# Adding the gated last row of v in the row tiles, by GpSimd from a broadcast half row, in a cross-attention and dense kernel

## What is computed

```python
q = layernorm(x);  k = v = ctx                       # 8 heads of 256 channels, 512 positions
corr = ifft(fft(q, positions) * conj(fft(k, positions))).real      # per channel
w, idx = top_k(corr, 12 per channel);  w = softmax(w)
out[pos] = sum_i w[i] * v[min(idx[i] + pos, 511)]    # per channel: shifted copies, clamped at the last row
x2 = x + tanh(g_xattn) * out
n = layernorm(x2)
base = n @ W_base.T + b_base
w_e = gates from softmax(n @ W_gate.T) and sigmoid(n @ W_thr + b_thr)
moe = (w_e * (n @ A_w[e].T)) @ B_w[e] summed over 8 experts, times 2
result = x2 + tanh(g_ffn) * (base + moe)
```

## Time and profile before

| | |
|---|---|
| median of 3 runs | 2907.98 us (2907.73 to 2909.68) |
| the profiled execution: its time / its span | 2908.95 us / 2907.1 us |
| busy: PE, PEld, DVE, ACT, POOL | 97%, 49%, 54%, 38%, 57% of the span |
| the attention's last output tiles end | at about 1318 us |
| first matmul of the first dense tile (L1146) | at 1381.65 us |
| mean granted clock of TensorE | 0.991 |

### The profile page before, as it was taken

The page is one execution under the profiler, slowest core; times in us unless marked ns, Lnnn a source line. Parts: engine busy times, 40 slices in busy tenths (PEclk is TensorE's granted clock), DMA queues, the critical chain, the costliest instruction groups (busy, mean ns, idle before and its releaser), DMA issues.

```text
span 2907.1 us, 35297 instructions
## 1 busy us (share of the span) xinstructions
PE 2815.5 (97%) x12932; PEld 1421.4 (49%) x12932; DVE 1559.7 (54%) x2646; ACT 1091.2 (38%) x1803; POOL 1661.9 (57%) x606
## 2 busy tenths in 40 slices
PE   5999999999999999987999999999999999999999
PEld 2454455555445555546444444444444444444444
DVE  5999999999999999996212112121212121212121
ACT  4666666666666664435211111111112121212110
POOL 4889898989898999950443343434242434333330
PEclk9999999999999999998999999999999999999999
DMA  5444445454444444347555454544444545445441
GB/s 199 131 131 125 131 138 143 145 145 140 121 122 136 134 131 116 102 160 259 167 169 159 148 155 159 152 161 149 159 144 160 152 158 157 153 159 156 148 131 44
DMA packets 264615, 424.97 MB, mean 146 GB/s; under 512 B 156271, under 2 KB 156847, under 8 KB 237109
## 3 DMA queue, kind: packets, MB, share of 16 engines
q1 hardware_dynamic: 245442, 288.93, 33.8%
q10 hardware_dynamic: 19068, 134.73, 13.4%
HBM read 256.79 MB, written 134.32 MB: 135 GB/s over the span
## 4 chain that ended last, share of the span: by engine, by line
PE 52%; DVE 24%; POOL 13%; issue 7%; DMA 2%; ACT 1%; DVEq 0%; ACTq 0%; POOLq 0%
PE bank L1146 42%; DVE top L773 2%; DVE rows_mem L1344 2%; DVE top L782 2%; DVE corr_mem L791 2%; POOL spec_o L916 2%; POOL rows_mem L875 2%; POOL rows_mem L891 2%; POOL v_odd L897 2%; POOL rows_mem L899 2%; POOL rows_mem L892 2%; POOL rows_mem L876 2%; DVE corr_mem L766 1%; PE bank L490 1%; DVE corr_mem L767 1%
## 5 line engine op out<-in xcount | busy, mean ns | idle before, releaser
L1337 DVE TENSOR_TENSOR hwt_lo<-bank,hwt_hi 128x128 f16<-128x128 f32 x32 | 9.3, 292 | 1075.0 <-ACT hwt_hi L1227 1075.0
L1369 POOL TENSOR_TENSOR rows_mem<-norm,rows_mem 128x2048 f16<-128x2048 f32 x31 | 126.1, 4067 | 696.4 <-ACT rows_mem L1208 696.4
L1146 PE MATMUL bank<-w_hi,rows_mem 128*128 128x512 f16 x2048 | 489.3, 379 | 3.8 <-DVE rows_mem L1344 3.8
L1146 PE MATMUL bank<-w_hi,parts_mem 128*128 128x512 f16 x2048 | 489.1, 379 | 3.6 <-DVE rows_mem L1344 3.6
L1227 ACT ACTIVATE hwt_hi<-bank 128x128 f16<-128x128 f32 x32 | 8.9, 277 | 933.8 <-PE bank L1154 908.6
L1146 PEld LDWEIGHTS bank<-w_hi,rows_mem 128*128 128x128 f16 x2048 | 200.4, 98 | 251.5 <-DVE rows_mem L1344 13.7
L1146 PEld LDWEIGHTS bank<-w_hi,parts_mem 128*128 128x128 f16 x2048 | 200.3, 98 | 250.8 <-DVE rows_mem L1344 12.8
L916 POOL TENSOR_TENSOR spec_o<-spec_o,term 128x1024 f32<-128x1024 f32 x127 | 297.7, 2370 | 33.0 <-DVE term L727 28.6
L1146 PE MATMUL bank<-w_lo,rows_mem 128*128 128x512 f16 x1024 | 262.8, 379 | 0.0
L1146 PE MATMUL bank<-w_lo,parts_mem 128*128 128x512 f16 x1024 | 262.8, 379 | 0.0
L490 PE MATMUL bank<-spec_o,table 128*128 128x512 f32 x512 | 251.2, 614 | 10.3 <-POOL spec_o L916 6.3
(11 more groups left out here) (204 smaller groups left out, 5180.6 us busy)
## 6 DMA issues: line engine op xcount, KB each, us to landing
rows_mem<-in_ctx_mirrored_dram SPq DMA_DIRECT2D x32, 1024.0 KB, 9.1
rows_mem<-in_x_mirrored_dram SPq DMA_DIRECT2D x32, 1024.0 KB, 10.4
parts_behind<-parts_mem SPq DMA_DIRECT2D x256, 128.0 KB
parts_ahead<-parts_mem SPq DMA_DIRECT2D x128, 256.0 KB
rows_mem<-x_scratch SPq DMA_DIRECT2D x32, 1024.0 KB, 4.8
rows_mem<-parts_behind ACTq DMA_DIRECT2D x32, 1024.0 KB, 5.9
out_dram<-rows_mem SPq DMA_DIRECT2D x32, 1024.0 KB, 3.9
norm<-in_x_dram ACTq DMA_DIRECT2D x31, 1024.0 KB, 5.8
```

Of the source, the lines that this page charges most:

```text
L1146: mm = pe.matmul(dense[o][:, :], nt(par, part)[:, k, :], w[:, k, o * 512:(o + 1) * 512], start=(k == 0 and n == 0), stop=False)
L1369: pool.tensor_tensor(norm_lo, norm[:, :], norm_hi, ALU.subtract).then_inc(norm_lo_made, 1)
```

## The change

The matmul L493 and its table go. ScalarE multiplies `last_raw` by tanh(g_xattn) once and stores it as `last_gated` (8 x 2048, f32) in DRAM. When a row tile is formed, the batch's row of it is broadcast to 128 partitions and GpSimd adds it: in the first tile as a whole row, loaded into the memory of the cosine part, and in the other 31 as two half rows of 1024 columns through one buffer `last_half`, loaded by ScalarE's queue and added one after the cosine part and one after the sine part. `last_added` takes the place of `formed` wherever a finished tile is waited for. The slots of `v_last` come free at `v_made` instead of `out_made`. The diff, without declarations and pure renames of arguments:

```diff
@@ SP: load_v_last, step, early_weights
                     if i >= 4:
-                        sp.wait_ge(out_made, 2 * (i - 3))
+                        sp.wait_ge(v_made, 4 * (i - 3))
...
                     if i == STEPS - 1:
-                        sp.wait_ge(formed, 2)
+                        sp.wait_ge(formed, 1)
+                        sp.wait_ge(gated_stored, 16)
+                        sp.dma_start(rows_mem[:, 0, :], last_gated[0:1].to_broadcast([128, D])).then_inc(first_last_loaded, 16)
+                        sp.wait_ge(last_added, 2)
                         sp.dma_start(x2_rows[0], norm[:, :]).then_inc(x2_kept, 16)
...
                     if m <= 1:
-                        sp.wait_ge(formed, 2)
+                        sp.wait_ge(last_added, 2)
@@ TensorE: out_tiles
                             mm = pe.matmul(to[:, part, :], o_tab[:, slot, :], spec_o[:, h, slot, :],
-                                           start=(row == 0), stop=(part == 1 and row == 1))
-                        if part == 0:
-                            mm = pe.matmul(to[:, 0, :], last_tab[:, 3, :], v_last[:, at, :], start=False, stop=True)
-                            if h == 0:
-                                mm.then_inc(cos_made, 1)
+                                           start=(row == 0), stop=(row == 1))
+                        if part == 0 and h == 0:
+                            mm.then_inc(cos_made, 1)
@@ ScalarE: before take_stats(NCH, 0)
+                act.activation(last_raw, last_raw, ACT.Copy, scale=gates[0:B * D // 256, 0:1]).then_inc(raw_gated, 1)
+                act.wait_ge(raw_gated, 1)
+                act.dma_start(last_gated.rearrange("b (q c) -> (b q) c", c=256), last_raw).then_inc(gated_stored, 16)
@@ GpSimd: first_tile
                     pool.tensor_tensor(norm[:, :], norm[:, :], rows_mem[:, 1, :], ALU.subtract).then_inc(formed, 1)
+                    pool.wait_ge(first_last_loaded, 16)
+                    pool.wait_ge(formed, 2)
+                    pool.tensor_tensor(norm[:, :], norm[:, :], rows_mem[:, 0, :], ALU.add).then_inc(last_added, 2)
@@ ScalarE: dense
+                def load_last(i, half):
+                    act.wait_ge(last_added, 2 * i + half)
+                    act.nop(nofuse=True)
+                    act.dma_start(last_half[:, :], last_gated[ds(i // TT, 1), half * (D // 2):(half + 1) * (D // 2)]
+                                  .to_broadcast([128, D // 2])).then_inc(last_loaded, 16)
+
                 def keep_x2(i, par):
-                    act.wait_ge(formed, 2 * (i + 1))
+                    act.wait_ge(last_added, 2 * (i + 1))
...
                         load_norm(i + 2)
+                        load_last(i + 2, 0)
                         if fleast(i) == 0:
                             hw_hi(i)
                         load_sine(i + 2, par)
+                        load_last(i + 2, 1)
                         keep_x2(i + 2, par)
@@ GpSimd: form
                     pool.wait_ge(norm_loaded, 32 * i)
                     pool.tensor_tensor(norm[:, :], norm[:, :], addend, ALU.add).then_inc(formed, 1)
+                    pool.wait_ge(formed, 2 * i + 1)
+                    add_last(i, 0)
                     pool.wait_ge(sine_loaded, 16 * i)
+                    pool.wait_ge(last_added, 2 * i + 1)
                     pool.tensor_tensor(norm[:, :], norm[:, :], addend, (ALU.subtract, ALU.add)[par]).then_inc(formed, 1)
+                    pool.wait_ge(formed, 2 * (i + 1))
+                    add_last(i, 1)
+
+                def add_last(i, half):
+                    cols = slice(half * (D // 2), (half + 1) * (D // 2))
+                    pool.wait_ge(last_loaded, 16 * (2 * (i - 1) + half + 1))
+                    pool.tensor_tensor(norm[:, cols], norm[:, cols], last_half[:, :], ALU.add).then_inc(last_added, 1)
```

27 lines of the change are left out of this document (18 added, 9 removed).

## The result

The changed kernel takes 2921.6 us (median of 5 runs, 2919.8 to 2922.6), the kernel before 2908.0 beside it (5 runs, 2906.8 to 2909.7). The ratio is 1.0046, 95% interval 1.0031 to 1.0060: **slower by 13.6 us**. That is inside the predicted range and 10 us above the forecast. The profiled execution of the changed kernel took 2920.75 us, its span is 2918.9 us, against 2907.1 before: 11.8 us more.

A forecast was written before the change was run, and what follows sets the result against it. TensorE was taken to bound the attention, VectorE less than 1 us behind, and the dense tiles; 2908.95 - 20 (attention) + 14 (seam) + 10 (first tiles) = 2912.95, less 0.97 to the median: 2912.0 us, range 2902 to 2923.

The forecast's parts named there:

- Part 1: Attention: removing the matmuls gains VectorE's waits for TensorE, 19 us, plus 1 us in the last step; sum -20.
- the last step: Last attention step: the removed matmul stands twice on the way to the last store, so 1 us more is gained.
- the seven special steps: Attention steps that carry a layer norm: VectorE is the bound there, so they give nothing of their own.
- Part 2: Seam before `correlate`: a third addition waits for a broadcast behind the store's DMAs, TensorE idles and its clock drops; +14 us.
- Part 3: Dense tiles: each of the first three forms adds to ScalarE's chain, plus a slower clock, +10 us; 28 later tiles 0.
- the 0.3 us that I took for sharing: First dense tiles: the half row's load, issued behind the x load, holds that load up by 0.3 us per link.
- even sharing: First dense tiles: upper bound, the half row holds up the x load by 1.6 us per link; cost 14 us.
- Later tiles: The 28 later dense tiles: 4.0 us in hand, of which the additions take 2.4, so they cost 0.
- (d): Later dense tiles: a form grows by over 4.0 us, `hw_hi` is late in each; over 2940 us; chance 0.05.
- (a): Seam and first-tile links are cheap: broadcast lands in 5 us, clock does not fall; 2902 us; chance 0.13.
- (b): Attention: TensorE does not set the pace, so removing matmuls gives nothing and the costs remain; 2932 us; chance 0.07.
- (c): Attention: tied engines' hand-overs add some 0.4 us to a step, so the gain is only 10; 2922 us; chance 0.15.

The follow-up runs named there:

- e12: The kernel before, unchanged, run once more for a second profile: 2908.1 us beside 2908.5.
- e1: The kernel before with the two last-row matmuls of each chunk left out and nothing in their place: 2898.9 us, ratio 0.9963.
- e10: e1 run once more, beside e9 and e11: 2898.3 us, ratio 0.9964.
- e2: e1, but the two matmuls kept in one step of four, the one ahead of TensorE's idle time: 2894.5 us, ratio 0.9949.
- e11: e2 run once more, beside e9 and e10: 2894.9 us, ratio 0.9954.
- e9: e2, but the two matmuls kept in the step right behind the one with TensorE's idle time: 2905.2 us, ratio 0.9990.
- e3: The changed kernel with the first tile's broadcast row loaded a step earlier, behind the tile's other loads: 2906.1 us, ratio 0.9990.
- e4: The changed kernel, but batch 0 keeps the matmuls, so only tiles 4 to 31 use additions: 2899.2 us, ratio 0.9968.
- e8: e4 plus two matmuls of a table of zeros in one step of four, ahead of TensorE's idle time: 2895.7 us, ratio 0.9962.
- e5: The changed kernel with the half row loaded only once for tiles 1 to 3, all six half additions using it: 2921.8 us, ratio 1.0048.
- e6: The changed kernel with the half additions of tiles 1 to 3 cut to one column, loads and waits kept: 2913.5 us, ratio 1.0021.
- e7: The changed kernel with the second half row of tiles 4 to 31 added twice: 2920.6 us, ratio 1.0046.

## Why the prediction was right or wrong

The stretches of all the profiles, worked out as in the first table:

| | before | e12 | after | e1 | e10 | e2 | e11 | e9 | e3 | e4 | e8 | e5 | e6 | e7 |
|---|---|---|---|---|---|---|---|---|---|---|---|---|---|---|
| attention | 1250.9 | 1250.9 | 1238.3 | 1236.3 | 1237.1 | 1236.5 | 1234.7 | 1243.6 | 1238.6 | 1238.6 | 1238.3 | 1238.4 | 1238.2 | 1238.3 |
| seam | 12.3 | 12.3 | 24.9 | 12.6 | 12.6 | 12.3 | 12.3 | 12.6 | 13.0 | 12.6 | 12.3 | 24.9 | 24.3 | 25.1 |
| weights | 112.0 | 110.8 | 111.7 | 115.0 | 111.7 | 111.0 | 110.3 | 111.4 | 109.3 | 111.8 | 110.1 | 113.6 | 112.5 | 111.5 |
| first tiles | 193.6 | 193.9 | 205.5 | 196.6 | 195.1 | 195.1 | 195.6 | 194.8 | 201.3 | 195.8 | 193.7 | 204.3 | 196.4 | 203.4 |
| later tiles | 1338.4 | 1338.5 | 1338.5 | 1338.5 | 1338.5 | 1338.5 | 1338.5 | 1338.5 | 1338.5 | 1338.5 | 1338.5 | 1340.2 | 1338.5 | 1339.8 |

**Part 1, the attention: the mechanism right, the size wrong** (-19 forecast for this stretch and -1 for the last step, -12.6 found; -9.5 and -9.8 for the whole of e1 and e10). TensorE did set the pace and VectorE did become the bound: ordinary steps are 37.6 to 38.0 us, one 38.3, where 37.7 was forecast. The 21 ordinary steps of the seven rounds went from 811.0 to 793.0 us, 18.0 less, and the forecast's way of counting has 16.4 + 21 x 0.09 = 18.3 for them. What failed is the sentence that the seven special steps "give nothing of their own": they went from 281.8 to 289.0 us and took 7.2 back. I had put that at nothing, and the 19 left 1.3 us for all new waits. Two things are in it. First, each special step is 0.5 to 0.6 us longer even at full clock (40.8 for 40.25), 3.9 in all: there TensorE, freed of two matmuls, only waits 1 us longer, and in the step behind it VectorE waits for TensorE. Second, the clock: slow special steps, 3.3 us in this profile (42.45, 42.11 and 41.2 against 40.8). 17.98 less 7.24 is the 10.7 between chunk 2 and chunk 30; the 1.9 from ahead of chunk 2, of which the forecast had 1.0 among its 23 waits, make it 12.6. e2, e9 and e11 show both by moving the matmuls to and from the idle time. The 1 us for the last step can't be told from the scatter of the stretch behind (109.3 to 115.0).

**Part 2, the seam: right** (+14 forecast; +12.7 to the start of `correlate` and 1.9 in it). Issue behind the 12 store DMAs, landing 8.1 us (forecast 7.9), the third addition ending 16.7 us behind the second (forecast some 17), `correlate` 8.98 us (forecast nearly 10). e3 shows the cause and its price.

**Part 3, the first tiles: right in what the additions cost, wrong in what else moves** (+10 forecast; +11.9 found). TensorE's idle time grew by 9.35 us where the forecast had 8.1, and the slower clock took 2.5 where it had 2. The place was another in the main: 6.4 us more ahead of tile 1's logits (7.60 for 1.20), and only 1.1 more ahead of its experts' matmuls (2.64 for 1.50), where the forecast had put all of it; the rest lies ahead of tile 2's. The three links, from the x load's issue to the third stored tile, are 108.1 us for 99.8, 8.3 longer. Of these 1.5 are the first x load, which landed after 11.0 us in place of 9.5; the other 6.8 are the additions, three of 2.4 us on paper, and e6 gives 8.1 in the times and 6.5 in the links. Kernels with these additions have 201.3 to 205.5 us in this stretch (four, mean 203.6), those without 193.7 to 196.6 (eight, mean 195.4): 8.2 us, less than the 10 I had. Another 1.6 us is what the forecast had no term for: the first tiles mostly come out that much longer behind the faster attention even without additions (e12), the x load landing after 10.5 us or more in place of 9.5, with a half row behind it or without. The changed kernel's profile is the highest of the four, 1.9 us above their mean, so scatter of that size is in the 11.9 too. On the 0.3 us that I took for sharing, the rule of the Trainium skill ("DMA: Bandwidth & Descriptors", section "Queues, rings and completion order"), that DMAs of one issuing engine are consumed in the order of its ring, is the better one: e5, with five of the six half rows gone, is no faster. The bound with even sharing (1.6 us per link) was far off.

**Later tiles: right, and safer than I said.** 28 tiles at 0 (the last stretch differs by 0.1 us, and e4 equals e1). Rival (d), that their room is used up at 4.0 us, had the wrong threshold: in e7 the form grew by 4.8 us and cost nothing.

**The rivals.** (a) *cheap seam*: wrong; e3 shows what a seam without the wait gives, with the first tiles as they are (2906). (b) *TensorE does not set the pace*: wrong, since e1 gains. The Trainium skill ("Trainium Kernel Development and Optimization", section "Performance Expectations") calls matmul busy time a bad metric and weight-load busy time a good one for how close a kernel is to roofline. Read as a measure of which engine sets the pace, as in the prediction, it would have missed this: weight loads filled 19.98 of 38.60 us, and TensorE was the bound all the same. (c) *only half comes back*, 2922 with a chance of 0.15: **its number came true, its mechanism only in part.** It had the hand-overs add 0.4 us to each step; ordinary steps show nothing of the kind, the special ones 0.5 to 0.6, and the clock and the first tiles did the rest. So the number was luck in part. What was there to be read in the trace before was TensorE's idle time of 1.10 us in each special step, which grows when TensorE comes earlier.

The working of the sum in the frame of one execution: -19 became -12.6, +14 became +14.6 (with `correlate`'s 1.9), +10 became +11.9, and the stretch between gave 2.1 back without that 1.9 (the last step's 1 us may be in it): 11.8, the difference of the two spans. The medians differ by 13.6, since the two profiled executions stand 1.0 above and 0.9 below their medians.

## What to carry to other kernels

When two engines are tied, an instruction's worth depends on the step it stands in: write down the round with every engine's waits, and count a removed instruction only where its engine does not wait that much longer behind it; idle time that grows can even bring a slower clock behind it (here in 21 of 62 places). Before a small operand is added to a late stage, look at where its DMA stands in the issuing queue: one load issued ahead of a store burst, in place of behind it, was worth 13.8 us of idle time and slow clock here, as much as the whole change lost. And where only a few iterations have no slack (here four of 32 tiles), keep the old way for these and use the new one for the rest.

## What the runs showed of the hardware

- TensorE's granted clock fell after 2.17 us of idling in some cases and not in others: two like places of the changed kernel read 0.62 (472 to 476 us) and 1.00 (164 to 168 us). Over nine kernels with 2.1 to 2.5 us of idling it was 21 of 62, over the four with 1.1 to 1.2 us (once 1.6) 0 of 28. More work for TensorE (e2, e11) made the kernel faster, and only a part of that gain is seen in this clock.
- A broadcast of one 8 KB row to 128 partitions landed in 8.1 us behind a store burst, as a full 1 MB load in that place (7.9 us). Half-row broadcasts of 512 KB landed in 3.4 to 15.5 us, and GpSimd waited for one in three cases only, 8.5 us in all:

```profile
  POOL norm L1412: 8.5, 3
...
DMA to landing us min/median/max: 3.4/5.3/15.5
```

(The rows are of line L1269 of the changed kernel: who waited for it, us and times, and the landing.)

- The same code between two like points took 201.3 to 205.5 us (first tiles with additions) or 109.3 to 115.0 us (weights) in the profiles of this study. In the weights the length goes with TensorE's granted clock over the stretch: 0.84 at 115.0 us (e1), 0.86 at 112.0 (before), 0.88 at 111.7 (after), 0.91 at 109.3 (e3). A difference of 2 us in one of these stretches of a single profile says little, and the kernel before had to be profiled a second time (e12) to tell that its early x load was not a single case.
